# Rank counts in two single-pass products a batch, spare products in the opening's waits, and one spare product a step in attention's last group

## The chip, the cores and the metric

The kernel runs on one core of one Trainium2 chip. The metric is device microseconds of that core, the median of several runs. The engines are TensorE (PE, its weight loads are listed as PEld), VectorE (DVE), ScalarE (ACT), GpSimd (POOL) and SyncE (SP). They run side by side and meet at semaphores.

## The reference

Four layers over `x` of 4 x 1024 x 128 (B = 4 batches, L = 1024 rows, D = 128), each added to its input after a layer norm:

```
x = x + _L0_attn_a_ref(_layernorm(x), ...)   # a rotation of each batch, a code-book term, RMS norm
x = x + _L0_ffn_ref(_layernorm(x), router_w, w1, w2)
x = x + _L0_attn_b_ref(_layernorm(x), ...)   # 16 heads of 8, softmax over 1024 keys
x = x + _L0_ffn_ref(_layernorm(x), router_w, w1, w2)
```

The feed-forward layer sends every row to two of eight experts:

```
logits = jnp.einsum('btd,ed->bte', x, router_w)
top_vals, top_idx = jax.lax.top_k(logits, K)          # K = 2
top_w = jax.nn.softmax(top_vals, axis=-1)
h = jnp.square(jax.nn.relu(jnp.einsum('nd,edh->enh', xf, w1)))
y = jnp.einsum('enh,ehd->end', h, w2)
out = ...sum over the two chosen experts of top_w * y
```

## The kernel before

The program is one long instruction list per engine, with stages in this order: an **opening** (first layer norm, the rotation's matrix, the RMS norm, and the routing of batches 0 and 1), **experts(0)** (the first feed-forward layer), **attention**, and **experts(1)** (the second one).

**Routing of one batch.** `turn_rows` turns the normed rows (`hbs`, tiles of 128) by transposes, ACT copies them out of PSUM, `batch_router` multiplies them by the router weights (`router`, eight products of 8 columns), and DVE copies the logits (`batch_top_two`), finds the largest two and marks them: `mark_two` writes `both`, 8 tiles x 8 experts of 0 or 1, with 8 zero columns behind. `batch_rank` (L1675) then counts on TensorE, for each row and expert, how many rows stand ahead. `rank_lines` (L1666) does that with one product by `tri` (a triangle of ones: rows ahead in the same tile) and eight products by `ones` (rows of all tiles ahead), product d shifted by d tiles and 8 columns narrower each time. All nine are fp32 and each shows as two weight loads and two matmuls in the trace. DVE turns the counts into destinations (`first_lines`, `line_places`), and POOL then **sends** the batch: 16 indirect DMAs that scatter `hbs` to `xs` in DRAM (L547). SP loads the sorted lines back (`load_lines`), and later POOL **fetches** the results by 16 indirect DMAs a batch (L553). A rank is taken eight times: batches 0 to 3 for each of the two feed-forward layers; in the second layer batch 0's lies inside attention (`fill_for_max`, task "rank"), batch 1's in the last group (`routed_late`), 2 and 3 in experts(1).

**experts(f)** walks 48 pairs of line tiles: `turn_lines` (L1704), `lines_hidden` (L1715, 256 columns, fp32), DVE's relu (`relu_pair`, L1332), `units_turned` (L1726), ACT's square (L903), `lines_result` (L1740).

**Attention** walks 16 groups of 16 steps (`STEPS`). A step s (kk is its place in the group) has four score products on 32 rows each (`scores`, L1896, 512 columns), ACT's four exponentials (L1008), sixteen products by the values (`times_values`, L1925), and for a later step the first pass over the scores for their maxima (`first_pass`, L1909, read by DVE's L1442). The first pass runs 13 steps ahead (`AHEAD`), so it ends three steps into the last group, and `routed_late(kk)` puts the routing of batches 1 and 2 of the second feed-forward layer in its place. PSUM slots for DVE (`sm`) alternate in the order of `bank_order`; slot `("out", 2 * GROUPS - 3)` is read at kk = 3 of the last group.

The order on each engine is that in which the code is written; nothing schedules it.

Of the kernel before, what the change touches and what calls it, by code (L numbers as in the profile page):

```python
# [14 lines left out]
P = 128  # L15
# [116 lines left out]
def hybrid_layer(nc, a, out):  # L132
    AR, DR = bank_order()
    ctx = ExitStack()
    with ctx:
# [40 lines left out]
        tri = sb("tri", [P, P])  # L176
# [61 lines left out]
        both = sb("both", [P, (TPB + 1) * E])  # L238
# [781 lines left out]
        def _(dve):  # L1020
# [80 lines left out]
            dve.memset(both[:, TPB * E:(TPB + 1) * E], 0.0)  # L1101
# [159 lines left out]
            def mark_two():  # L1261
                io = iota[:, 0:E].rearrange("p (o e) -> p o e", o=1).broadcast_to([P, TPB, E])
                for k in range(2):
                    ins = dve.tensor_tensor(hot[:, k], io, ixfb[:, :, k:k + 1].broadcast_to([P, TPB, E]), ALU.is_equal)
                link(ins)
                return dve.tensor_tensor(both[:, 0:TPB * E].rearrange("p (t e) -> p t e", e=E), hot[:, 0], hot[:, 1],
                                         ALU.add)
# [274 lines left out]
        def _(pe):  # L1542
# [123 lines left out]
            def rank_lines(bank, parts=(0, 1)):  # L1666

                if 0 in parts:
                    pe.matmul(bank, tri[:], both[:], start=True, stop=False, skip_group_check=True)
                for part in parts:  # L1670
                    for d in range(TPK * part + 1, TPK * (part + 1) + 1):
                        ins = pe.matmul(bank[:, d * E:], ones[:], both[:, 0:(TPB + 1 - d) * E], start=False,  # L1672
                                        stop=(d == TPB), skip_group_check=True)
                return ins
# [111 lines left out]

            def experts_begin():
# [9 lines left out]
                pe.wait_ge(G_("cbb_ready"), 1)  # L1797
                for u in range(2):
                    turn_rows(0, 0, u)
                pe.wait_ge(G_("wqk_loaded"), 48)  # L1800
                batch_router(0, 0)
                second_rows(NBLK - 1)
                batch_rank(0, 0)
                for u in range(2):
                    turn_rows(0, 1, u)
                batch_router(0, 1)
                batch_rank(0, 1)
                pe.wait_ge(G_("w1_loaded"), 16)
                pe.wait_ge(G_("w2_loaded"), 16)

            def routed_late(kk):
# [9 lines left out]
                elif kk in (13, 14):  # L1821
                    batch_router(1, 2, (kk - 13,))

# [156 lines left out]
            for s in range(STEP0, STEP1):  # L1980
# [18 lines left out]
                if s // STEPS == GROUPS - 1:  # L1999
                    routed_late(s % STEPS)  # L2000
# [69 lines left out]
```

## Time and profile before

| | us |
|---|---|
| median of 3 runs | 1381.24 (1376.31 to 1381.48) |
| the profiled execution, its own time | 1387.96 |
| its span | 1386.1 |
| PE busy, PEld busy | 1099.2, 634.3 |
| DVE, ACT, POOL busy | 891.8, 767.9, 540.6 |
| mean granted TensorE clock | 0.865 of full |

The times in rows are microseconds from the span's start. In the timeline a row gives start, duration, engine, line, operation, tiles written and read, shape and count; in brackets stands how long the engine had been idle and what ended that. "remote" there, and "another core or an unknown queue" in the chain, is a wait whose end no instruction of the trace explains. A granted clock of 1.00 is 2.4 GHz, 0.50 is 1.2 GHz; these are the only two levels in the trace.

### The profile page before, as it was taken

Reading aid. Unit: us, or ns where it says so; the run is one execution under the profiler, and the core shown is the slowest. Engines: PE = TensorE matmul, PEld = TensorE weight load, DVE = VectorE, ACT = ScalarE, POOL = GpSimd, SP = SyncE. Lnnn points to the kernel's source line nnn. Section 1 sums busy time; section 2 is a strip of 40 time slices with the busy share of each in tenths; the row PEclk is TensorE's granted clock in tenths of the full one; section 3 lists DMA queues with packets and bytes.
Section 4 is the critical chain, followed back from the end, with each engine's and each line's share of the span. In section 5 each row is a group of like instructions: output and inputs, shape, how many; then the busy total and the mean of one; then the engine's idle time right before and its main releaser. Section 6 shows DMA issues by size and latency. Waiting matters only on the chain.

```text
span 1386.1 us, 23924 instructions
## 1 busy us (share of the span) xinstructions
PE 1099.2 (79%) x8950; PEld 634.3 (46%) x8950; DVE 891.8 (64%) x1819; ACT 767.9 (55%) x1508; POOL 540.6 (39%) x626
## 2 busy tenths in 40 slices
PE   2745765698799999999999999999999688666660
PEld 1444664586233434343444444344343337655560
DVE  6584421346788899998888898888899214223132
ACT  3311221243288888888878888888889322212220
POOL 2035435426745543243424333333221441235344
PEclk9856877797599999999999999999999558778885
DMA  5602313132000000000000000000000102132323
GB/s 192 194 16 79 93 53 104 52 104 61 22 9 9 2 1 2 1 1 1 1 2 1 2 1 2 1 1 1 1 2 2 61 31 85 49 96 65 99 62 109
DMA packets 74863, 57.87 MB, mean 42 GB/s; under 512 B 7676, under 2 KB 68223, under 8 KB 74623
## 3 DMA queue, kind: packets, MB, share of 16 engines
q1 hardware_dynamic: 66558, 39.55, 9.6%
q0 software_dynamic: 8192, 16.79, 4.1%
q8 instruction: 74, 1.21, 0.4%
q14 instruction: 39, 0.31, 0.1%
HBM read 27.68 MB, written 28.57 MB: 41 GB/s over the span
## 4 chain that ended last, share of the span: by engine, by line
PE 58%; DVE 19%; another core or an unknown queue 9%; issue 7%; ACT 4%; POOL 1%; DMA 1%; SPq 0%; POOLq 0%; DVEq 0%; ACTq 0%
PE acc L1925 16%; DVE mxp L1442 10%; PE six L1896 9%; PE six L1715 5%; PE misc L1896 5%; PE six L1726 3%; PE acc L1740 3%; ACT PB L1008 2%; PE six L1740 2%; PE six L1909 1%; PE six L1636 1%; PE six L1704 1%; PE six L1862 1%; PE six L1672 1%
## 5 line engine op out<-in xcount | busy, mean ns | idle before, releaser
L1442 DVE TENSOR_REDUCE mxp<-six 128x2 f32<-128x1024 f32 x512 | 599.0, 1219 | 82.9 <-PE six L1909 71.9
L1008 ACT ACTIVATE PB<-six 128x512 f32<-128x512 f32 x675 | 381.9, 599 | 94.9 <-PE six L1896 47.3
L1925 PE MATMUL acc<-PB,Vg 128*32 128x256 f32 x4096 | 340.8, 405 | 21.4 <-ACT SC L995 14.5
L1896 PE MATMUL six<-Q,K 32*128 32x512 f32 x675 | 280.5, 511 | 4.4 <-issue 4.3
L1909 PE MATMUL six<-K,Q 32*128 32x512 f32 x1024 | 264.3, 516 | 19.5 <-DVE mxp L1442 12.6
L1332 DVE TENSOR_SCALAR PB<-six 128x512 f32<-128x512 f32 x96 | 63.9, 669 | 292.0 <-PE six L1715 135.3
L1008 ACT ACTIVATE PB<-misc 128x512 f32<-128x512 f32 x349 | 208.8, 598 | 51.3 <-PE six L1896 26.4
L903 ACT ACTIVATE PB<-six 128x512 f32<-128x512 f32 x96 | 55.8, 581 | 298.5 <-remote 172.0
L547 POOL DMA_INDIRECT xs<-hbs,dest x128 | 123.8, 967 | 155.9 <-DVE dest L1305 119.2
L1896 PE MATMUL misc<-Q,K 32*128 32x512 f32 x349 | 178.3, 511 | 7.6 <-ACT PB L1008 6.8
L1896 PEld LDWEIGHTS six<-Q,K 32*128 32x128 f32 x675 | 111.8, 187 | 154.6 <-issue 80.0
L637 POOL TENSOR_TENSOR tr<-SC,cst 128x512 fp32r<-128x512 f32 x64 | 66.7, 1042 | 287.3 <-ACT SC L862 287.3
L1925 PEld LDWEIGHTS acc<-PB,Vg 128*32 128x32 f32 x4096 | 83.5, 110 | 151.5 <-issue 82.9
L1726 PE MATMUL six<-cst,PB 128*128 128x128 f32 x368 | 64.7, 303 | 103.1 <-issue 48.8
L553 POOL DMA_INDIRECT hbs<-yd,dest x96 | 91.6, 954 | 108.1 <-issue 91.2
L1909 PEld LDWEIGHTS six<-K,Q 32*128 32x128 f32 x1024 | 97.6, 188 | 35.3 <-DVE mxp L1442 24.3
L1715 PE MATMUL six<-w1s,VH 128*128 x368 | 107.0, 415 | 3.4 <-issue 3.1
L1726 PEld LDWEIGHTS six<-cst,PB 128*128 128x128 f32 x368 | 50.2, 156 | 120.5 <-issue 69.1
L1896 PEld LDWEIGHTS misc<-Q,K 32*128 32x128 f32 x349 | 65.3, 187 | 82.0 <-ACT PB L1008 50.5
L1715 PEld LDWEIGHTS six<-w1s,VH 128*128 128x128 f32 x368 | 69.5, 211 | 10.6 <-issue 4.4
L1740 PE MATMUL acc<-w2s,PB 128*128 x384 | 61.1, 311 | 1.8 <-issue 1.8
L1740 PEld LDWEIGHTS acc<-w2s,PB 128*128 128x128 f32 x384 | 57.0, 227 | 0.7 <-issue 0.7
(310 smaller groups left out, 1307.7 us busy)
## 6 DMA issues: line engine op xcount, KB each, us to landing
yd<-PB SPq DMA_DIRECT2D x40, 256.0 KB
xs<-turned SPq DMA_DIRECT2D x4, 1472.0 KB, 12.2
K<-xs SPq DMA_DIRECT2D x20, 256.0 KB
Q<-xs SPq DMA_DIRECT2D x20, 256.0 KB
x<-in_x SPq DMA_DIRECT2D x4, 512.0 KB, 6.9
SC<-in_w_om SPq DMA_DIRECT2D x1, 2048.0 KB, 12.9
xs<-hbs,dest POOLq DMA_INDIRECT x128
out<-x SPq DMA_DIRECT2D x8, 256.0 KB
```

The lines of the kernel that those rows point to most:

```text
L547: pl.indirect_dma_start(xs[b], bass.IndirectOffsetOnAxis(ap=dest[:, b, k, i:i + 1], axis=0), hbs[:, b, i, :], None).then_inc(G_(f"sent{b}" ...
L553: pl.indirect_dma_start(lines_back[b][:, k, i, :], None, yd[b], bass.IndirectOffsetOnAxis(ap=dest[:, b, k, i:i + 1], axis=0)).then_inc(G_( ...
L637: pl.tensor_tensor(tr[:, task % 2, :], qf[:, task % 2, :], mask.broadcast_to([P, BLK]), ALU.mult).then_inc(G_("high_masked"), 1)
L1008: act.activation(PB[:, s % 3, j, :], scores, ACT.Exp).then_inc(G_("act_taken"), 1)
L1332: dve.tensor_scalar(rls[:, n % 2, 0:w], big[:, n % 2, 0:w], 0.0, None, ALU.max).then_inc(G_("rlp_done"), 1)
L1442: dve.reduce_max(dst, taken_slot("max", s, i).rearrange("p (a n) -> p a n", a=2), AX.X).then_inc(G_("max_taken"), 1)
L1715: ins = pe.matmul(big[:, n % 2, r % 2 * HID:(r % 2 + 1) * HID], hTs[:, group % 2, r % TG * P:(r % TG + 1) * P], w1s[:, ds(expert_at[b, r], ...
L1726: ins = pe.transpose(unit_bank[:, k * P:(k + 1) * P], rls[:, n % 2, k * P:(k + 1) * P], ident)
L1740: ins = pe.matmul(result_bank(group)[:, r % TG * D:(r % TG + 1) * D], sqs[:, n % 3, at:at + P], w2f[:, ds(expert_at[b, r] + c * D, D)], st ...
L1896: pe.matmul(bank, K[rows, G % NG, t * P:(t + 1) * P], Q[rows, G % NG, u * BLK:(u + 1) * BLK], start=True, stop=True).then_inc(G_("act_fill ...
L1909: ins = pe.matmul(slot[:, c * BLK:(c + 1) * BLK], Q[rows, G % NG, t * P:(t + 1) * P], K[rows, G % NG, th * BLK:(th + 1) * BLK], start=True ...
L1925: ins = pe.matmul(acc[RB * j:RB * (j + 1), n], Vg[:, G % 2, t, j, :], PB[:, s % 3, j, n], start=(t == 0 and half == 0), stop=(t == TPB - 1 ...
```

## The change

There are three parts.

**Ranks.** `mark_two` writes `marks` (fp32r, 8 zero columns ahead and behind the 64) and then, by three more adds on DVE, sums over two, four and eight tiles: `twos`, `fours`, `ahead`. `rank_lines` is then two products of 72 columns in fp32r: `tri` by `marks` and `ones_r` by `ahead`, one in each part. `tri` becomes fp32r. In the opening one memset becomes two memsets and two copies.

**Spare products in the opening.** `spare_rows(count, width)` multiplies rows of `hTa` into PSUM bank `six[:, 1]` (fp32, 512 or 256 columns); nobody reads them. The first eight come behind a wait for the second block of the RMS norm (`t_ready` 2), ahead of the first `turn_rows`.

**Spare products in the last group.** `keep_awake` is one fp32r product of 512 columns from kk = 4 on, 12 in all, ahead of `routed_late`; at kk = 4 PE waits for the slot to be read.

```diff
@@ mark_two
-                return dve.tensor_tensor(both[:, 0:TPB * E].rearrange("p (t e) -> p t e", e=E), hot[:, 0], hot[:, 1],
-                                         ALU.add)
+                n = TPB * E
+                link(dve.tensor_tensor(marks[:, E:E + n].rearrange("p (t e) -> p t e", e=E), hot[:, 0], hot[:, 1], ALU.add))
+                marked = marks[:].bitcast(F32)
+                link(dve.tensor_tensor(twos[:, 2 * E:], marked[:, E:E + n], marked[:, 0:n], ALU.add))
+                link(dve.tensor_tensor(fours[:, 4 * E:], twos[:, 2 * E:], twos[:, 0:n], ALU.add))
+                return dve.tensor_tensor(ahead[:, E:], fours[:, 4 * E:], fours[:, 0:n], ALU.add)
@@ rank_lines
-                    pe.matmul(bank, tri[:], both[:], start=True, stop=False, skip_group_check=True)
-                for part in parts:
-                    for d in range(TPK * part + 1, TPK * (part + 1) + 1):
-                        ins = pe.matmul(bank[:, d * E:], ones[:], both[:, 0:(TPB + 1 - d) * E], start=False,
-                                        stop=(d == TPB), skip_group_check=True)
+                    ins = pe.matmul(bank, tri[:], marks[:, E:], start=True, stop=False, skip_group_check=True)
+                if 1 in parts:
+                    ins = pe.matmul(bank, ones_r[:], ahead[:], start=False, stop=True, skip_group_check=True)
@@ new
+            def spare_rows(count, width=BLK):
+                for _ in range(count):
+                    pe.matmul(six[:, 1, 0:width], hTa[:, 0:P], hTa[:, 0:width], start=True, stop=True)
@@ experts_begin, PE
+                pe.wait_ge(G_("t_ready"), 2)
+                spare_rows(8)
                 for u in range(2):
                     turn_rows(0, 0, u)
+                    spare_rows(1, BLK // 2)
...
                 batch_rank(0, 0)
+                spare_rows(8)
                 for u in range(2):
                     turn_rows(0, 1, u)
+                    spare_rows(1, BLK // 2)
                 batch_router(0, 1)
+                spare_rows(3)
                 batch_rank(0, 1)
+                spare_rows(4)
@@ attention's steps, PE
+                    if s % STEPS == 4:
+                        pe.wait_ge(*max_taken("out", 2 * GROUPS - 3))
+                    if s % STEPS >= 4:
+                        keep_awake()
                     routed_late(s % STEPS)
@@ new
+            def keep_awake():
+                bank = sm[:, DR["out", 2 * GROUPS - 3] % 2, 0:BLK]
+                pe.matmul(bank, wkh[:, 0, :], hTh[:, 0:BLK], start=True, stop=True)
```

TensorE in the opening before, from the rank of batch 0 to the first lines of experts(0). `tr` holds the turned rows, `K` the sorted lines:

```order
L1669 MATMUL six<-both,tri 128x72
L1672 MATMUL six<-both,ones 128x64
...
L1672 MATMUL six<-both,ones 128x8
L1647 MATMUL misc<-cst,hbs 128x128 x8
L1652 MATMUL six<-rwf,tr 128x8 x8
L1669 MATMUL six<-both,tri 128x72
L1672 MATMUL six<-both,ones 128x64
...
L1672 MATMUL six<-both,ones 128x8
L1690 TENSOR_LOAD tw
L1704 MATMUL six<-cst,K 128x128 x4
```

The same stretch now (L1799 are the spare products, reading `hTa`, which lies in `PB`):

```order
L1680 MATMUL six<-marks,tri 128x72
L1682 MATMUL six<-ahead,ones_r 128x72
L1799 MATMUL six<-PB 128x512 x8
L1658 MATMUL misc<-cst,hbs 128x128 x4
L1799 MATMUL six<-PB 128x256
L1658 MATMUL misc<-cst,hbs 128x128 x4
L1799 MATMUL six<-PB 128x256
L1663 MATMUL six<-rwf,tr 128x8 x8
L1799 MATMUL six<-PB 128x512 x3
L1680 MATMUL six<-marks,tri 128x72
L1682 MATMUL six<-ahead,ones_r 128x72
L1799 MATMUL six<-PB 128x512 x4
```

The nine products of each rank have become two, and 15 spare ones (and two halves) stand in this stretch; four of them stand between the second rank and the first lines.

TensorE in the last group before, around the first part of batch 1's rank (`routed_late(10)`):

```order
L1896 MATMUL six<-Q,K 128x512 x2
L1647 MATMUL six<-cst,hbs 128x128 x4
L1669 MATMUL six<-both,tri 128x72
L1672 MATMUL six<-both,ones 128x64
L1672 MATMUL six<-both,ones 128x56
L1672 MATMUL six<-both,ones 128x48
L1672 MATMUL six<-both,ones 128x40
L1925 MATMUL acc<-PB,Vg 32x256 x4
```

And now, with the `keep_awake` product (L1851) ahead of the turned rows:

```order
L1925 MATMUL six<-Q,K 128x512 x2
L1851 MATMUL six<-hTh,wkh 128x512
L1658 MATMUL six<-cst,hbs 128x128 x4
L1680 MATMUL six<-marks,tri 128x72
L1954 MATMUL acc<-PB,Vg 32x256 x4
```

One product of 512 columns came in, four of the five rank products of this part went out.

DVE around the marking of batch 0 before, and now:

```order
L1264 TENSOR_TENSOR hot<-cst,ixfb 128x64 x2
L1266 TENSOR_TENSOR both<-hot 128x64
L1271 TENSOR_SCALAR eds<-ed 128x8
```

```order
L1271 TENSOR_TENSOR hot<-cst,ixfb 128x64 x2
L1274 TENSOR_TENSOR marks<-hot 128x64
L1276 TENSOR_TENSOR twos<-marks 128x64
L1277 TENSOR_TENSOR fours<-twos 128x64
L1278 TENSOR_TENSOR ahead<-fours 128x64
L1282 TENSOR_SCALAR eds<-ed 128x8
```

One add has become four in a chain, ahead of everything else on DVE.

## Rows read from the trace of the kernel before

**Rows 1.** The page, part 4: shares of the chain that ended last
```profile
PE 58%; DVE 19%; another core or an unknown queue 9%; issue 7%; ACT 4%; POOL 1%; DMA 1%; SPq 0%; POOLq 0%; DVEq 0%; ACTq 0%
```
**Rows 2.** Timeline of the opening: routing of batch 0, start, duration, what
```profile
67.10 0.48 PE L1796 MATMUL misc<-Vg,ones 1*128 1x128 f32 x2 [2.54 <-ACT Vg L931]
...
73.87 1.09 PE L1647 MATMUL misc<-cst,hbs 128*128 128x128 f32 x4 [6.29 <-DVE hbs L1232]
...
82.11 0.22 DVE L1253 COPY lgb<-six 128x64 f32<-128x64 f32 x1
...
85.49 0.23 DVE L1266 TENSOR_TENSOR both<-hot 128x64 f32<-128x64 f32 x1
...
85.78 0.70 PE L1669 MATMUL six<-both,tri 128*128 128x72 f32 x2 [3.40 <-DVE both L1266]
...
86.15 3.53 PEld L1672 LDWEIGHTS six<-both,ones 128*128 128x128 f32 x16
...
89.89 0.17 DVE L1289 TENSOR_SCALAR tilesi<-six 128x8 int32<-128x8 f32 x1 [3.65 <-PE six L1672]
...
92.88 1.16 POOL L547 DMA_INDIRECT xs<-hbs,dest  x1 [9.15 <-DVE dest L1305]
```
**Rows 3.** Timeline of the opening: routing of batch 1 and the first relu
```profile
112.84 0.23 DVE L1253 COPY lgb<-six 128x64 f32<-128x64 f32 x1 [8.40 <-remote]
...
124.98 0.98 POOL L547 DMA_INDIRECT xs<-hbs,dest  x1 [9.36 <-DVE dest L1305]
...
128.10 1.29 DVE L1332 TENSOR_SCALAR PB<-six 128x512 f32<-128x512 f32 x2
```
**Rows 4.** Windows: stretch, its length, PE busy (count), granted clock, DMA share, GB/s
```profile
65.00:70.00 5.00, 0.48 (x2) 0.93 0.46 131
...
150.00:155.00 5.00, 5.00 (x38) 0.88 0.17 52
```
```profile
1080.00:1085.00 5.00, 3.34 (x17) 0.50 0.16 54
...
1120.00:1125.00 5.00, 5.00 (x30) 0.50 0.13 42
```
**Rows 5.** Timeline of experts(0): a pair of 256-column products at either clock; a rank
```profile
124.37 1.91 PE L1715 MATMUL six<-w1s,VH 128*128 x4
...
127.40 1.03 PE L1715 MATMUL six<-w1s,VH 128*128 x4
...
153.85 0.34 PE L1669 MATMUL six<-both,tri 128*128 128x72 f32 x2
...
153.97 1.87 PEld L1672 LDWEIGHTS six<-both,ones 128*128 128x128 f32 x16
```
**Rows 6.** The chain that ended last, in the last group: start, duration, what
```profile
1109.49 1.65 PE six L1672 x8
...
1115.66 1.81 PE six L1672 x8
...
1120.21 0.72 PE misc L1896
```
**Rows 7.** Timeline of the last group: POOL's sends and ACT's unexplained waits
```profile
1092.90 0.96 POOL L547 DMA_INDIRECT xs<-hbs,dest  x1 [0.31 <-issue]
...
1096.74 0.60 ACT L1008 ACTIVATE PB<-misc 128x512 f32<-128x512 f32 x1 [8.26 <-remote]
```
```profile
1120.46 0.96 POOL L547 DMA_INDIRECT xs<-hbs,dest  x1 [26.60 <-DVE dest L1305]
...
1139.43 0.96 POOL L547 DMA_INDIRECT xs<-hbs,dest  x1 [0.30 <-issue]
...
1143.32 0.60 ACT L1008 ACTIVATE PB<-six 128x512 f32<-128x512 f32 x1 [7.29 <-remote]
```
**Rows 8.** Timelines of experts(1): a rank at full clock, one with the clock low
```profile
1158.38 1.03 PE L1672 MATMUL six<-both,ones 128*128 128x64 f32 x8
...
1162.34 0.96 PE L1672 MATMUL six<-both,ones 128*128 128x32 f32 x8
```
```profile
1237.72 1.86 PE L1672 MATMUL six<-both,ones 128*128 128x64 f32 x8
...
1243.91 0.96 PE L1672 MATMUL six<-both,ones 128*128 128x32 f32 x8
```
**Rows 9.** POOL's own timeline: first sends or fetches of a series in both expert stages
```profile
162.53 0.97 POOL L547 DMA_INDIRECT xs<-hbs,dest  x1 [15.28 <-DVE dest L1305]
201.61 0.98 POOL L553 DMA_INDIRECT hbs<-yd,dest  x1 [19.13 <-issue]
```
```profile
1169.59 0.96 POOL L547 DMA_INDIRECT xs<-hbs,dest  x1 [29.20 <-DVE dest L1305]
...
1250.33 1.00 POOL L547 DMA_INDIRECT xs<-hbs,dest  x1 [19.52 <-DVE dest L1305]
```

More of the change, by code:

```diff
@@ L175, in hybrid_layer @@
         hbs = sb("hbs", [P, B, TPB, D])
-        tri = sb("tri", [P, P])
+        tri = sb("tri", [P, P], F32R)
         ident = cst[:, C_ID:C_ID + P]
@@ L237, in hybrid_layer @@
         hot = sb("hot", [P, 2, TPB, E])
-        both = sb("both", [P, (TPB + 1) * E])
+        marks = sb("marks", [P, (TPB + 2) * E], F32R)
+        twos = sb("twos", [P, (TPB + 2) * E])
+        fours = sb("fours", [P, (TPB + 4) * E])
+        ahead = sb("ahead", [P, (TPB + 1) * E], F32R)
         upto = sb("upto", [P, E, E])
@@ L1100, in _ @@
             link(dve.tensor_tensor(om_skew[:], s1[0:OD, 1, 0:OD], om_bias[:], ALU.subtract))
-            dve.memset(both[:, TPB * E:(TPB + 1) * E], 0.0)
+            dve.memset(twos[:], 0.0)
+            link(dve.memset(fours[:], 0.0))
+            dve.tensor_copy(marks[:], fours[:, 0:(TPB + 2) * E])
+            dve.tensor_copy(ahead[:], fours[:, 0:(TPB + 1) * E])
             dve.tensor_tensor(upto[:], iota[:, 0:E].rearrange("p (e o) -> p e o", o=1).broadcast_to([P, E, E]),
@@ L1797, in experts_begin @@
                 pe.wait_ge(G_("cbb_ready"), 1)
+                pe.wait_ge(G_("t_ready"), 2)
+                spare_rows(8)
                 for u in range(2):
                     turn_rows(0, 0, u)
+                    spare_rows(1, BLK // 2)
                 pe.wait_ge(G_("wqk_loaded"), 48)
-                batch_router(0, 0)
+                batch_router(0, 0, (0,))
+                spare_rows(1, BLK // 2)
+                batch_router(0, 0, (1,))
                 second_rows(NBLK - 1)
+                spare_rows(1)
                 batch_rank(0, 0)
+                spare_rows(8)
                 for u in range(2):
                     turn_rows(0, 1, u)
+                    spare_rows(1, BLK // 2)
                 batch_router(0, 1)
+                spare_rows(3)
                 batch_rank(0, 1)
+                spare_rows(4)
                 pe.wait_ge(G_("w1_loaded"), 16)
```

## The prediction

> **What bounds the kernel now.** I read the chain that ended last first. TensorE has 58% of it, DVE 19%, and 9% is put down to nothing in the trace [rows 1]. So the mean busy shares decide little; I went by places. The timeline around POOL's indirect DMAs explains the 9%. A series of 16 sends takes about 20 us (from 1120.46 to the end of the last send, 1139.43 + 0.96), and while it runs some engine stops without a cause in the trace and goes on 2.9 us after the last send: ACT at 1096.74 after 8.26 us, with the last send over at 1093.86, and at 1143.32 after 7.29 us, with the last over at 1140.39 [rows 7]. DVE's wait of 8.40 us that ends at 112.84 lies at the end of the first series in the same way [rows 2, 3]. I take from this, as an inference, that **work done during a series is covered, and work between the end of a series and the start of the next is paid in full**. A series of sends starts when DVE has the destinations, which hang on a rank. So for each edit I ask whether it lies between series.
>
> The clock is the second view. It is low from about 69 to 125 us (the first row of [rows 4] shows the fall) and again from 1080 to 1145: 13 windows of 5 us at 0.50, of which the first and one in the middle stand in [rows 4]. In the second of them TensorE is busy 5.00 of 5.00 us and the clock stays at 0.50.
>
> **Rank of batch 0, opening.** Before: `both` ends at 85.72, and DVE reads the counts at 89.89, 4.17 us later [rows 2]. Now: three more adds of 0.23 us [rows 2] with some 0.03 between them, 0.8 us, then two single-pass products of 72 columns. The trace has no such pair. Its nearest rows are the two passes of one fp32 product of 72 columns: 0.34 us at full clock [rows 5] and 0.70 at half [rows 2]; I take 0.6 with the handover. 4.17 - 0.8 - 0.6 = 2.8 us saved (2.7 to 3.0), and the sends at 92.88 hang on it: **-2.8**.
>
> On weights, the trace and a rule differ. The 16 weight loads of the eight `ones` products take 3.53 us at half clock and 1.87 at full [rows 2, 5], 221 and 117 ns each. The Trainium skill, TensorE: Matmul & The Clock Gate, section LDWEIGHTS, prices a load of 128 columns at about 107 ns whatever the clock. By that the 18 loads of this rank would be 1.9 us, and this term about -1.1 in place of -2.8; I go by the rows.
>
> **Rank of batch 1.** DVE computes statistics of batch 2 while TensorE ranks, so the rank is hidden and only the three adds count, on the way to the sends at 124.98 [rows 3]: **+0.8**.
>
> **Ranks in the expert stages.** At full clock a rank is 0.34 + 1.9 us [rows 5]; two products are about 0.5, so 1.7 saved. Batch 2's (153.85) lies between series, with TensorE busy 5.00 of 5.00 us [rows 4] and sends at 162.53 [rows 9]: **-1.7**. Batch 3's lies inside the fetches that begin at 201.61 [rows 9]: 0. In the second layer batch 2's (1158 and 1162 [rows 8]) lies before the sends at 1169.59: **-1.7**. Batch 3's takes 1.86 + 0.96 and its `tri` product, some 3.2 us, before the sends at 1250.33 [rows 8, 9]: **-2.2** (-2.7 less a part for the added DVE work). Any of these can be worth 0 if DVE or ACT is late next; that is the lower bound of each.
>
> **Rank inside attention.** TensorE and DVE are both close to full there; the products give 1.7 and the adds cost 0.8. From +0.8 to -1.7; I take **-0.5**.
>
> **Last group.** What is paid is from ACT's return at 1096.74 to the sends at 1120.46. The chain there is TensorE, at half clock. The rank's 1.65 + 1.81 and its `tri` product, 3.8 us [rows 6], become 0.6: -3.2. Four `keep_awake` products (kk 8 to 11) come in. A score product of the same 512 columns has 0.72 in the chain [rows 6]; 0.43 is its columns at 1.2 GHz. I take 0.6: +2.4. Together **-0.8**. The other eight lie at kk 4 to 7, before and in the first series, and at kk 12 to 15, inside the second: cover is the engine stop of 8.26 and of 7.29 us [rows 7]. If that cover goes they cost 8 x 0.72 = 5.8 more. The one at kk 4 is ahead of the first sends: **+0.4**. The wait at kk 4 is for a slot that DVE reads at kk 3, long before: 0.
>
> **Spare products in the opening.** A pair of 256-column fp32 products takes 1.03 us at full clock and 1.91 at half [rows 5], so one of 512 columns about 0.85 and 1.71 in a row of many. The first eight start behind 67.6 [rows 2]. Before, the clock falls in the window up to 70 us, in which TensorE worked 0.48 of 5 us [rows 4]; with products in that idle time I expect it to stay up, and eight take 6.8 us, to 74.8, against a need at 73.87 [rows 2]. DVE takes the logits only at 82.11 [rows 2], and they are ready 2 us before, so 1 us late costs nothing: 0. The eight behind the first rank end before the rows of batch 1 are ready, the three lie in DVE's unexplained wait. The last four stand ahead of the first lines, 3.4 to 6.8 us; DVE is not ready for the first relu before 128.10 [rows 3], TensorE has 1.8 us to spare there and gains some 1.8 us more at full clock: 0 (to +1.7). The two memsets and copies lie in a wait of DVE: 0.
>
> **Sum.** -2.8 + 0.8 - 1.7 - 1.7 - 2.2 - 0.5 - 0.8 + 0.4 = -8.5 us. I take off a sixth for what DVE or ACT will hold back once TensorE is shorter: -7. The profiled execution took 1387.96, its span and 1.9 us around it, 0.5% above the median; it would become 1381, and the median 1381.24 becomes **1374**.
>
> **The rivals.**
> *The clock comes back early in the last group.* If the added product brings it to 1.00 soon after 1097, the 23 us up to the sends shrink, ACT's exponentials (four of 0.60 us a step [rows 7]) becoming the bound near 15 us: 8 more, **1366**. Against it: busy 5.00 of 5.00 us at 0.50 [rows 4], and the added product takes time of its own.
> *The savings are taken back.* The series of sends and fetches, not the ranks, set the pace, and each saving lengthens an unexplained wait. Then only the opening's 2.8 less 0.8 and the added products count, about **1381**. For it: batch 3's rank already lies in a series.
> *Slower: spare products at half clock with their cover gone.* Places: the first eight in the opening, the four ahead of the first lines, kk 4 to 7 and 12 to 15 of the last group. If the clock falls at 69 us in spite of them, the first eight take up to 13.7 us, to 81.3; the turned rows are then 7.4 us late, 5.4 after the 2 us to spare. The four cost the 1.7 of their bound, and the eight of the last group 8 x 0.72 = 5.8 at half clock if no stop covers them. 1374 + 5.4 + 1.7 + 5.8 = **1387**. It decides from the point where the first eight take over 8 us. For it: the clock is low in both places before [rows 4].
>
> **How the numbers follow.** Forecast 1374 (1369 to 1379) 0.50; clock back early 1366, 0.15; taken back 1381, 0.15; slower 1387, 0.20. About 0.5% (7 us) is what a measurement can tell from no change. The forecast lies at that edge: I give 0.30 of its 0.50 to faster, which with the second case makes 0.45; 0.35 for the same; 0.20 slower. The range takes in the middle of the fast and of the slow case: 1363 to 1387.
>
> **What would show it.** Right: the counts are read under 1.6 us after the marks, the first sends begin near 90, each rank is two matmul records; the clock is 1.00 from 67 us until the second rows; ACT's return in the last group still follows the last send by 2.9 us. Wrong: the first turned rows begin after 76; an unexplained wait at a new place between series, since every engine's instruction list has shifted; or the clock at 1.00 between 1100 and 1120.

## The result

The changed kernel took **1373.72 us** (median of 20 runs, 1367.68 to 1377.32); the kernel before, run beside it, 1381.01 (20 runs, 1369.87 to 1389.49). The ratio is 0.9949, 95% interval 0.9932 to 0.9966: 7.3 us less. The profiled execution took 1372.43 with a span of 1370.6, 1.3 us below its median; that of before was 6.9 above its later median. So of the 15.5 us between the two spans, 8.2 are chance, and where that chance lies in the traces isn't known; my estimate is that a single term can be read to some 2 us at best.

The chain of the changed kernel, from its page, part 4, answers to [rows 1]; the share with no cause in the trace rose from 9 to 11%:

```profile
PE 56%; DVE 20%; another core or an unknown queue 11%; issue 6%; ACT 4%; POOL 1%; DMA 1%; SPq 0%; POOLq 0%; DVEq 0%; ACTq 0%
```

The opening of the changed kernel, from the timelines of TensorE, DVE and POOL (start, duration, line and operation, idle time before it), answers to [rows 2] and [rows 3]:

```profile
66.95 8.83 PE L1799 MATMUL six<-PB 128*128 128x512 f32 x16 [0.36 <-ACT cbb L936]
75.61 0.60 PE L1658 MATMUL misc<-cst,hbs 128*128 128x128 f32 x4
...
80.85 0.22 DVE L1259 COPY lgb<-six 128x64 f32<-128x64 f32 x1
...
84.25 0.22 DVE L1274 TENSOR_TENSOR marks<-hot 128x64 fp32r<-128x64 f32 x1
...
85.31 0.43 PE L1680 MATMUL six<-marks,tri 128*128 128x72 f32 x1 [3.05 <-DVE ahead L1278]
85.54 0.41 PE L1682 MATMUL six<-ahead,ones_r 128*128 128x72 f32 x1
...
86.06 0.17 DVE L1300 TENSOR_SCALAR tilesi<-six 128x8 int32<-128x8 f32 x1 [0.28 <-PE six L1682]
...
89.04 1.16 POOL L550 DMA_INDIRECT xs<-hbs,dest  x1 [6.55 <-DVE dest L1316]
...
111.72 0.22 DVE L1259 COPY lgb<-six 128x64 f32<-128x64 f32 x1 [11.13 <-remote]
...
122.94 0.98 POOL L550 DMA_INDIRECT xs<-hbs,dest  x1 [11.19 <-DVE dest L1316]
```

From the end of the marks (84.47) to the read of the counts (86.06) it is 1.59 us; it was 4.17. The first send came 3.84 us earlier than in [rows 2], but 1.26 of that was there already at the copy of the logits (80.85 against 82.11), which no part of the change explains.

The last group of attention, from POOL's and ACT's timelines, answers to [rows 7]:

```profile
1084.95 0.96 POOL L550 DMA_INDIRECT xs<-hbs,dest  x1 [0.30 <-issue]
...
1088.60 0.60 ACT L1011 ACTIVATE PB<-misc 128x512 f32<-128x512 f32 x1 [10.28 <-remote]
...
1110.88 0.96 POOL L550 DMA_INDIRECT xs<-hbs,dest  x1 [24.97 <-DVE dest L1316]
```

ACT comes back 2.7 us after the last send is over (1085.91) and the next sends follow 22.3 us later; before, these were 2.9 and 23.7. The windows of the changed kernel (stretch, length, busy time and count of TensorE, its weight loads, DVE, ACT and POOL, granted clock, DMA share, GB/s) answer to [rows 4]:

```profile
65.00:70.00 5.00, 3.54 (x7) 1.76 (x8) 4.47 (x30) 1.32 (x10) 0.19 (x1) 0.78 0.34 96
70.00:75.00 5.00, 5.00 (x11) 2.08 (x11) 4.76 (x22) 0.00 (x0) 0.38 (x1) 0.88 0.00 0
...
85.00:90.00 5.00, 4.69 (x7) 2.27 (x8) 4.21 (x22) 0.00 (x0) 0.96 (x1) 0.50 0.01 2
...
95.00:100.00 5.00, 4.66 (x31) 3.63 (x30) 4.66 (x23) 1.19 (x2) 3.78 (x5) 1.00 0.15 52
...
1095.00:1100.00 5.00, 5.00 (x29) 2.04 (x25) 1.09 (x6) 1.97 (x5) 0.00 (x0) 0.50 0.01 3
1100.00:1105.00 5.00, 5.00 (x26) 2.88 (x22) 0.00 (x0) 2.55 (x6) 0.00 (x0) 0.50 0.00 0
```

The chain that ended last in that group, in order of time (start, duration, what), answers to [rows 6]:

```profile
1095.89 0.72 PE six L1851
...
1100.94 0.73 PE six L1851
...
1102.52 0.06 PE six L1680
...
1107.09 0.72 PE six L1851
1107.82 0.06 PE six L1682
```

In the opening the clock comes and goes. In the last group it stays at the 1.2 GHz level from ACT's return to the sends, with a `keep_awake` in each step.

### The profile page after: what moved, and what is told of

Same layout as the page of the kernel before. It is cut to its first block, busy times and chain, and to the rows that moved or that the text cites. A ratio compares the mean times of both kernels' runs of the same rounds, so it can differ in the third digit from the quotient of the medians.

```text
span 1370.6 us, 23835 instructions
## 1 busy us (share of the span) xinstructions
PE 1109.0 (81%) x8892; PEld 622.7 (45%) x8892; DVE 896.8 (65%) x1846; ACT 766.7 (56%) x1508; POOL 539.6 (39%) x626
## 4 chain that ended last, share of the span: by engine, by line
PE 56%; DVE 20%; another core or an unknown queue 11%; issue 6%; ACT 4%; POOL 1%; DMA 1%; SPq 0%; POOLq 0%; DVEq 0%; ACTq 0%
PE acc L1954 16%; DVE mxp L1453 10%; PE six L1925 9%; PE six L1724 5%; PE misc L1925 5%; PE six L1735 3%; PE acc L1749 3%; ACT PB L1011 2%; PE six L1749 2%; PE six L1647 1%; PE six L1891 1%; PE six L1713 1%; PE six L1938 1%; DVE PB L1343 1%
## 5 line engine op out<-in xcount | busy, mean ns | idle before, releaser
L906 ACT ACTIVATE PB<-six 128x512 f32<-128x512 f32 x96 | 55.7, 580 | 286.2 <-remote 163.4
L1925 PEld LDWEIGHTS six<-Q,K 32*128 32x128 f32 x675 | 112.0, 187 | 153.0 <-issue 77.7
L678 POOL TENSOR_TENSOR Q<-turned,Q 128x512 fp32r<-128x512 f32 x32 | 40.8, 1276 | 41.1 <-ACT turned L986 41.1
```

Of the source, the lines that this page charges most:

```text
L1925: pe.matmul(bank, K[rows, G % NG, t * P:(t + 1) * P], Q[rows, G % NG, u * BLK:(u + 1) * BLK], start=True, stop=True).then_inc(G_("act_fill ...
```

## The experiments

**Two kinds of chip.** The result stands on a chip whose engines stop during the series of indirect transfers. Eleven of the twelve experiments ran on two other chips, where they do not, and there the kernel before takes some 1190 us in place of 1381. The last ran on a chip that has the stops, where before takes 1390.73. That was chance, and it made two questions of one: what each part is worth with the stops, and without them.

On the chips without stops, executions of one kernel also fall into two clusters. Of the 78 of before, 37 lie between 1182 and 1193 with a mean granted clock of 0.931, and 41 between 1193 and 1204 with 0.918. The difference of 0.013 over 1190 us is about 30 us at half speed, which is how long the clock is low in the last group in the trace of before from the upper cluster (1198.25). So medians there depend on how many executions fall on which side, and the ratios, made against before's own mixture, do not rank the kernels as the medians do. I read places instead. "Sends (1,0)" are those of the second layer's batch 0, and so on; **D** is the distance from the first of them to the start of the last long series of transfers, 80 in a row, after which the kernel needs 111 to 112 us whatever was done before. Each of these distances is from one profiled execution. "At half clock" is the time that TensorE's granted clock stood at 0.50 between 990 and 1060 us.

| kernel | products of 512 columns in the last group | median, us (runs) | at 1193 or more | at half clock, us | sends (1,0) to (1,1), us | (1,0) to (1,2), us | D, us |
|---|---|---|---|---|---|---|---|
| before | none | 1196.97 (35), 1188.0 (18), 1195.98 (25) | 41 of 78 | 34.2 | 29.5 | 67.3 | 90.7 |
| ranks_only | none | 1190.17 (12) | 2 | 23.8 | 26.4 | 59.4 | 82.8 |
| no_keep | none | 1192.42 (12) | 5 | 30.7 | 26.1 | 62.0 | 85.9 |
| no_keep_b (same) | none | 1187.63 (10) | 2 | 13.6 | 23.8 | 55.5 | 79.5 |
| half_sends | none | 1186.97 (1) | | 20.5 | 25.2 | 58.1 | 81.6 |
| no_spares | one a step | 1188.87 (12) | 4 | 0 | 23.0 | 53.0 | 76.5 |
| after_again | one a step | 1183.84 (10) | 3 | 0 | 23.1 | 53.1 | 76.5 |
| old_ranks | one a step | 1189.10 (12) | 0 | 0 | 24.8 | 56.6 | 81.8 |
| keep_two | two a step | 1187.50 (10) | 0 | 0 | 24.7 | 55.7 | 79.1 |
| keep_early | four in steps 8, 9, 10 | 1185.38 (10) | 0 | 6.8 | 23.9 | 55.5 | 79.0 |
| keep_late | four in steps 12, 13, 14 | 1187.64 (10) | 1 | 10.2 | 25.2 | 56.7 | 80.1 |

In the four kernels with the new ranks and no products the distance (1,0) to (1,2) grows by 0.38 us for each us at half clock, and all four lie on that line within 0.1 us. Followed down to no time at half clock it gives 50.3 us, an estimate; with twelve products and the clock kept it is 53.0 to 53.1. So the products cost some 2.7 us there, and pay where the clock would else be low for more than some 7 us.

D leaves out what lies ahead of it, and there the changed kernel gained nothing on these chips: its first sends of all come 2 us earlier (91.47 in after_again against 93.42 in before_again), but sends (1,0) come 2.2 us later (996.19 against 994.01).

### First set: one part at a time

These expectations were written for a chip with the stops.

**ranks_only**: the changed kernel without the spares and without `keep_awake`.

```
-                pe.wait_ge(G_("t_ready"), 2)
-                spare_rows(8)
...
-                    if s % STEPS >= 4:
-                        keep_awake()
```


> The changed kernel without any spare product: no spare_rows in the opening and no keep_awake in attention's last group; only the ranks in two products. Theory (the ranks carry the gain, the spare products are nearly free or a cost): the first sends begin at about 90 us as in the changed kernel, and the section from ACT's return to the sends of batch 1 in the last group is 2.9 us shorter than in the changed kernel, because four keep_awake products of 0.72 us are gone from a chain at half clock. Time 1371, ratio to before 0.993, so 2 to 3 us better than the changed kernel. Rival (the spare products carry it by the clock): the opening after 67 us stays at 0.50 and loses what they gave, time 1378 to 1381, ratio 0.998 or more.

Measured: 1190.17 us (1183.87 to 1193.83), ratio 0.9967 (0.993 to 1.0004), and by medians 1.3 us above no_spares and 6.3 above after_again, where 2 to 3 us below the changed kernel was expected. D is 7.9 us shorter than before's. Both had lost the clock in the last group, but for 24 us here and 34 there: at 0.38 us for each us that is an estimate of 4 us for the clock, and leaves 4 us for the two ranks that lie in D, those of batches 1 and 2, a part of them at half clock.

**no_keep**: the same with the opening's spares.

```
-                    if s % STEPS >= 4:
-                        keep_awake()
```


> The changed kernel without keep_awake: ranks in two products and the opening's spare products. Theory: as the granted clock was 0.50 in the last group with them too, they only cost 0.72 us each where TensorE is the chain, kk 8 to 11: 2.9 us less between ACT's return and the sends of batch 1. Time 1371, ratio 0.9925. Rival (they are covered, or they keep some stretch at full clock): the same time as the changed kernel, ratio 0.995, or slower.

Measured: 1192.42 us (1184.53 to 1197.92), ratio 1.0001 (0.9959 to 1.0044): not the 0.9925 of the theory. Against ranks_only the spares gave nothing by the times.

**no_spares**: the changed kernel without the opening's spares, with `keep_awake`.

```
-                spare_rows(8)
...
-                spare_rows(4)
```


> The changed kernel without the opening's spare products: ranks and keep_awake. Theory (they lie in waits and the clock they give is spent waiting for VectorE): the first sends begin within 1 us of the changed kernel's, ratio 0.995 as the changed kernel. Rival (the full clock in the opening is worth something): the transposes and the router products of batch 0 run at half clock, 3.4 us of products take twice as long, the first sends come 1 to 3 us later and the ratio is 0.997.

Measured: 1188.87 us (1176.33 to 1201.33), ratio 0.9928 (0.9881 to 0.9975). The first sends come at 91.43, as in after_again (91.47): the theory, not the rival.

**old_ranks**: the kernel before, with its nine products a rank, plus both kinds of spare products.

```
+                pe.wait_ge(G_("t_ready"), 2)
+                spare_rows(8)
...
+                    if s % STEPS >= 4:
+                        keep_awake()
```


> The kernel before with both kinds of spare products and the old ranks in nine fp32 products each. Theory: no gain, since the ranks carry it; keep_awake costs 2.9 us in the last group, the opening's rank now runs at whatever clock the eight products ahead of it leave. Time 1382 to 1385, ratio 1.001 to 1.003. Rival (spare products matter): ratio 0.997 or less.

Measured: 1189.10 us (1185.44 to 1192.93), ratio 0.9978 (0.9944 to 1.0012), between the 1.001 of the theory and the 0.997 of the rival, and the interval holds both. Against after_again, with the clock at 2.4 GHz in both, the sends of batch 1 come 1.7 us later after those of batch 0 and the sends of batch 2 1.8 us later after those of batch 1, with one rank in each stretch: **1.7 to 1.8 us a rank**, the 1.7 of the prediction. The rest of the 5.3 us in D, 1.8, lies between the sends of batch 2 and the last series and stays unexplained; batch 3's rank comes after D's end.

What I had not expected stood in the windows of the last group. ranks_only, without the products:

```profile
1005.00:1010.00 5.00, 4.91 (x30) 2.35 (x30) 3.49 (x32) 3.08 (x7) 3.78 (x5) 0.54 0.15 52
1010.00:1015.00 5.00, 5.00 (x29) 2.17 (x27) 0.31 (x2) 3.15 (x7) 3.78 (x5) 0.50 0.15 52
```

no_spares, with one a step:

```profile
1005.00:1010.00 5.00, 4.62 (x45) 2.04 (x37) 3.55 (x33) 3.51 (x8) 3.78 (x5) 1.00 0.15 52
1010.00:1015.00 5.00, 5.00 (x44) 2.54 (x43) 0.58 (x4) 4.40 (x9) 3.40 (x4) 1.00 0.16 54
```

TensorE is busy 4.6 to 5.0 of 5 us in both, and in the one the clock falls. The prediction had the products as a cost alone.

### Second set: is it the products?

**before_again** and **after_again** are the two kernels unchanged; **no_keep_b** is no_keep once more.

> The kernel before, unchanged, for its trace beside the others of this set. Theory (the clock of attention's last group decides what the changed kernel gains): where the engines do not stop during the first series of sends of the second layer, TensorE falls to the 1.2 GHz level some 10 us after the first send of that group's batch 0 and runs 20 us or more there, as in the kernel with the ranks alone (1008 to 1038 us); the first sends of batches 0 and 1 are about 26 us apart and those of batches 1 and 2 about 33. Rival (the ranks alone decide it): the clock is at 2.4 GHz there. Whether the stops named in the prediction are there at all is read here too: with them a series of 16 indirect transfers is followed by at least 7 us without one in all seven places of the experts' stage of layer 2, and the time is about 1381; without them that stage has one series of 80 transfers, and the time is about 1190.

Measured: 1198.25 us, one run. No stops: the last stage has one series of 80. The clock is at half from 1005 us for more than 30 us, as the theory has it, and D is 90.7. The sends are 29.5 and 37.8 us apart, more than the 26 and 33 expected, which were read from the kernel with the new ranks. From its windows:

```profile
1005.00:1010.00 5.00, 5.00 (x32) 1.70 (x26) 1.51 (x15) 2.30 (x6) 3.78 (x5) 0.50 0.17 56
...
1020.00:1025.00 5.00, 5.00 (x33) 1.67 (x32) 3.53 (x17) 2.10 (x4) 1.22 (x2) 0.50 0.04 12
```


> The changed kernel, unchanged. If there are no stops: the clock stays at 2.4 GHz through attention's last group, the second layer's sends of batches 0, 1 and 2 start about 23 and 30 us apart, and the time is 8 us (0.7%) below before's, within 4; the rival (four products a batch is all cost, 0.6 to 0.7 us each) expects 2 to 3 us more than the same kernel without them. If there are stops, as in the profiles shown: 7 us (0.5%) below before's, and the clock does not come back before the second series ends.

Measured: 1183.84 us (1181.64 to 1200.83), ratio 0.9968 (0.9919 to 1.0018), 4.2 us below before's 1188.0 by medians and not clear of noise, so the 8 us are not shown by the times; the sends are 23.1 and 30.0 us apart as expected. From its windows:

```profile
1005.00:1010.00 5.00, 4.62 (x36) 2.78 (x36) 2.90 (x30) 4.28 (x10) 3.83 (x4) 1.00 0.17 56
...
1020.00:1025.00 5.00, 5.00 (x44) 2.96 (x36) 0.83 (x4) 3.77 (x9) 3.78 (x5) 1.00 0.66 189
```


> The changed kernel without the one product of 512 columns a step in attention's last group; the spares of the opening and the new ranks stay. Theory without stops: the clock is lost from about 1008 us for 20 us or more, and the kernel is 3 to 9 us slower than the changed one. With stops: the clock is lost with and without the products, they are a cost of 0.72 us each, and this kernel is about 3 us faster than the changed one. Rival (the products never matter): within 1 us of the changed one.

Measured: 1187.63 us (1184.16 to 1194.54), ratio 0.9999 (0.9954 to 1.0044), 3.8 us above after_again by medians, D 3.0 longer. The clock was lost at 1005 us again, but came back after some 7 us and was lost once more: without the products the loss has no fixed length (D 79.5 here, 85.9 in the same kernel of the first set), which fits the 6 us between the two profiles of one kernel.

### Third set: how many, and where

**keep_two**: two products a step.

```
                         keep_awake()
+                        keep_awake()
```


> Two products of 512 columns a step in attention's last group in place of one, the rest as in the changed kernel. On a chip without stops each product takes 0.34 us of TensorE's path at 2.4 GHz, so twelve more cost 4.1 us. Theory (the products hold the clock, and the executions of the changed kernel near 1198 us are those in which it was lost all the same): no execution is 10 us above the fastest, the median is 1187, from 1185 to 1189, against 1184 for the changed kernel, clock at 2.4 GHz from 1000 to 1045 us. Rival (those executions have another cause): some 3 in 10 stand 12 us above the rest as with one product. With stops: the clock still does not come back before the second series of sends ends, and the time is 3 us above the changed kernel's for some four more products at 0.72 us.

Measured: 1187.50 us (1182.65 to 1189.65), ratio 0.995 (0.9908 to 0.9991): the 1187 of the theory, and no execution of ten at 1193 or more. The clock is at 2.4 GHz from 1000 to 1045 us in the profiled execution. The price of one product at full clock is read from TensorE's timeline of after_again:

```profile
1005.54 0.50 PE L1851 MATMUL six<-hTh,wkh 128*128 128x512 f32 x1
1005.87 0.95 PE L1663 MATMUL six<-rwf,tr 128*128 128x8 f32 x8
```

0.33 us from start to start, 4 us for twelve; keep_two's median is 3.7 us above after_again's. That the second product is what keeps executions away from 1198 us is not shown: old_ranks, with one product a step, has none of 12 at 1193 or more, and the kernels with the new ranks and no products have 9 of 34.

**keep_early**: ranks_only with the twelve products in steps 8, 9 and 10.

```
-                    if s % STEPS >= 4:
-                        keep_awake()
+                    if s % STEPS in (8, 9, 10):
+                        for _ in range(4):
+                            keep_awake()
```


> The new ranks without the opening's spares; the products of 512 columns not one a step but four in each of steps 8, 9 and 10 (as many, twelve), which is about 1005 to 1013 us, where the kernel without products loses the clock. Theory (what decides is that TensorE has wide products where the clock falls): the first loss at 1005 us does not come or comes some us later, the clock may fall after 1018 us, and the first two series of sends are 24 us apart. Rival (any twelve products do): at 2.4 GHz all through, as with one a step, series 23 us apart.

Measured: 1185.38 us (1181.70 to 1189.54), ratio 0.9979 (0.9941 to 1.0016), none of ten at 1193 or more. The clock holds at 1005 us and falls at 1020, and the first two series are 23.9 us apart, all as in the theory. From its windows:

```profile
1005.00:1010.00 5.00, 5.00 (x41) 3.07 (x43) 1.08 (x6) 3.37 (x7) 3.78 (x5) 1.00 0.15 52
...
1020.00:1025.00 5.00, 5.00 (x31) 2.90 (x34) 0.00 (x0) 1.89 (x4) 3.77 (x5) 0.52 0.12 42
```

**keep_late**: the same with `(12, 13, 14)`.

> The same with the twelve products in steps 12, 13 and 14, about 1018 to 1024 us, after the place at which the clock is lost. Theory: it falls near 1005 us as without products and stays at 1.2 GHz at least to 1013 us; the first two series of sends are 26 us apart or more; the time is 3 to 9 us above that of the kernel with the products in steps 8 to 10. Rival (any twelve do): the same as that kernel within 1 us.

Measured: 1187.64 us (1182.90 to 1193.07), ratio 0.9952 (0.991 to 0.9994). The first two series are 25.2 us apart, a little under the 26 expected. The clock falls at 1005 us, is back at 1014.7, before the first of the products at 1018.28, and then stays up. From its windows, and from TensorE's timeline:

```profile
1005.00:1010.00 5.00, 5.00 (x32) 1.72 (x27) 2.20 (x18) 2.30 (x6) 3.78 (x5) 0.50 0.15 52
...
1015.00:1018.00 3.00, 3.00 (x31) 1.23 (x29) 1.52 (x8) 2.47 (x6) 0.00 (x0) 1.00 0.41 124
...
1020.00:1025.00 5.00, 5.00 (x46) 2.90 (x42) 0.80 (x4) 2.57 (x6) 3.78 (x5) 1.00 0.21 67
```
```profile
1018.28 1.20 PE L1842 MATMUL six<-hTh,wkh 128*128 128x512 f32 x4
```

So the products did not bring the clock back: it came back without any, as in no_keep_b (1011.8) and half_sends (1013.4). What they did is keep it there. All profiled kernels of the chips without stops agree on this. At 1005 us the six without such products up to that point lost the clock (before_again, ranks_only, no_keep, no_keep_b, half_sends, keep_late) and the five with them did not. Between 1020 and 1030 us it is low, for a part or all of that time, in the five kernels without them and in keep_early, whose products are over by then, and at 1.00 in the five that have them there, keep_late among them. What counts is the place; "any twelve do" falls, though by times keep_early and keep_late are only 2.3 us apart, less than the 3 to 9 expected and within their spread.

**half_sends**: ranks_only, and of the 16 sends of batch 1 in the second layer only eight.

```
+                if f and b == 1:
+                    last = TPB // 2
```

The two waits that count these transfers are lowered by as much.

> The new ranks alone (no spares, no products in attention's last group), and of the 16 sends of batch 1 in the second layer only the first 8: rows of four of its eight tiles are not sent, so that part of the output is left out. Theory on a chip without stops (from batch 2's sends on, GpSimd's issue of 80 transfers, 1.27 us each, paces the end, and what goes before only shifts its start): the series of batch 1 takes 10 us instead of 20; the last series starts at the usual distance from batch 2's sends, and the kernel is 0 to 4 us faster than with all sends, since batch 2's rank and router, not POOL, are late there. Rival (POOL's transfers pace attention's last group too): 10 us faster. With stops: the engines stop 10 us instead of 20 after this series began, and the time falls by 10 us.

Measured: 1186.97 us, one run, against 1190.17 for all sends, within the 0 to 4 us expected. The next series starts 33.0 us after, as in ranks_only (32.9), though POOL had been free for 23 us:

```profile
1050.79 0.96 POOL L552 DMA_INDIRECT xs<-hbs,dest  x1 [23.19 <-DVE dest L1318]
```

So POOL's series does not pace attention's last group. The experts' stage after it is another matter. POOL's timeline of after_again, its first and one of its last transfers:

```profile
1072.70 1.00 POOL L556 DMA_INDIRECT hbs<-yd,dest  x1 [3.55 <-issue]
...
1173.99 0.94 POOL L556 DMA_INDIRECT hbs<-yd,dest  x1 [0.30 <-issue]
```

There the series lasts 102.2 us in before_again and in after_again, so the rank of batch 3 inside it gives nothing.

### Fourth: two products and no spares, on a chip with stops

**two_no_spares**: keep_two without the opening's spares.

```
-                spare_rows(8)
...
                         keep_awake()
+                        keep_awake()
```


> The changed kernel with two products of 512 columns a step in attention's last group in place of one, and without the opening's spares. Theory (the opening's clock buys nothing, since DVE's chain and the 16 transfers of a series pace the sends there, and what it would save before 100 us is taken back in the first layer's experts): the mark reads still come 1.6 us after the counts' marks, the first series of sends starts within 1 us of the kernels with spares (90 to 92.5 us), the clock is at 1.2 GHz from 80 to 100 us, and the median is that of the kernel with spares and two products, 1187.5, within 2 us. Rival (the spares carry the opening): first sends 2 us later and the median 1189.5 or more. Both expect no execution 10 us above the fastest. With stops: 3 us below before's time.

Measured: 1381.24 us (1379.56 to 1385.63, 6 runs) against 1390.73 for before beside it: ratio **0.9942** (0.992 to 0.9964), the same gain as the change as a whole on its chip, and 9.5 us where 3 were expected. The counts are read 1.59 us after the marks and the first sends start at 91.77, as the theory has it. From its timelines, DVE in the opening and ACT in the last group:

```profile
111.67 0.22 DVE L1259 COPY lgb<-six 128x64 f32<-128x64 f32 x1 [8.35 <-remote]
```
```profile
1093.91 0.60 ACT L1011 ACTIVATE PB<-misc 128x512 f32<-128x512 f32 x1 [8.25 <-remote]
```

And its windows of the last group, to be set beside those of the changed kernel above:

```profile
1100.00:1105.00 5.00, 5.00 (x26) 2.17 (x21) 1.75 (x12) 1.94 (x4) 0.00 (x0) 0.50 0.00 0
1105.00:1110.00 5.00, 5.00 (x43) 2.41 (x41) 0.00 (x0) 3.75 (x8) 0.00 (x0) 0.91 0.01 3
1110.00:1115.00 5.00, 5.00 (x41) 2.18 (x45) 3.47 (x17) 3.62 (x8) 0.95 (x1) 1.00 0.00 0
```

With two products a step the clock comes back 12 us after ACT's return, and the sends of batch 1 start 43.1 us after those of batch 0 (1070.9 and 1114.05), against 45.1 with one product and 46.7 in the kernel before, which has none and the old ranks. That is the rival "the clock comes back early"; it gave 2 us in place of 8, since the return came late. That the second product brought it is likely but not shown: it is one trace, on another chip than the changed kernel's.

**The spares of the opening.** They buy nothing there. From the normed rows (`hbs`) to the copy of the logits it is 9.49 us with them (after_again, clock 0.82 to 1.00 from 80 to 95 us) and 9.50 without (no_spares, clock 0.50), and DVE waits for nothing at that copy: its own work sets it. The first sends come at 91.47 and 91.43. In batch 1 they shorten the way from `hbs` to the copy from 7.49 to 6.36 us; with stops DVE waits there for something else in any case, and the copy comes at 111.72 with them and at 111.67 without. Later they cost: from the first sends to those of batch 2 it is 54.4 to 54.5 us in the five kernels with spares on the chips without stops, and 53.1 to 53.2 in the five with the new ranks and no spares. By times they made no gain (no_keep against ranks_only), and with the stops the gain was whole without them, though with a second product a step in the last group.

## Why the prediction was right, point by point

The time (1373.7 for a forecast of 1374), the range and the leaning to faster by a little held. The terms did less well than their sum. They add up to -8.5 us, of which I took off a sixth for no row that I could name; the places in the two traces add up to the 15.5 us between the spans, of which 8.2 are chance. That the median fell on the forecast to 0.3 us is in part luck.

- **Rank of batch 0, -2.8: right.** 4.17 us became 1.59, 2.6 saved; on the chips without stops 4.17 (before_again) became 1.58 (no_spares). With the price that the Trainium skill, TensorE: Matmul & The Clock Gate, section LDWEIGHTS, gives a load of 128 columns, the term would have been an estimate of -1.1; the 221 ns a load at half clock and the 2.6 us saved decide against that.
- **Rank of batch 1, +0.8: right without the spares.** From the copy of the logits to the first send it is 13.7 us in before_again (106.02 to 119.76) and 14.3 in no_spares (104.04 to 118.36); with the stops 12.1 in [rows 3] and 12.9 in two_no_spares (111.67 to 124.61). In the changed kernel's own trace it is 11.2, the other sign; why stays open.
- **Ranks in the expert stages, -1.7 and -1.7 for batch 2: right in size.** From batch 1's sends to batch 2's it is 1.5 us less in the first layer and 1.6 in the second (0.8 and 1.2 in two_no_spares).
- **Batch 3's ranks, 0 and -2.2: both mis-sized, and the 0 is a step that failed.** In the first layer its rank starts at 205.39, inside the fetches that begin at 201.61 [rows 9], and I took it as covered. From the start of those fetches to batch 3's sends it was 29.9 us (231.50); it is 26.9 in the changed kernel (198.25 to 225.15) and 27.0 in two_no_spares: **3.0 us saved for the 0 forecast**. The place is a relu of DVE behind the stop, ahead of the destinations, first before's, then the changed kernel's:

```profile
229.73 0.69 DVE L1332 TENSOR_SCALAR PB<-six 128x512 f32<-128x512 f32 x1 [2.68 <-PE six L1715]
```
```profile
223.39 0.69 DVE L1343 TENSOR_SCALAR PB<-six 128x512 f32<-128x512 f32 x1
```

Before, TensorE's hidden products for it came only after the stop, and DVE waited 2.68 us; now they are there, in two_no_spares (227.71) too. So work inside a series counts where it decides how far TensorE is when the stop begins. That the shorter rank is what brings it further is likely, but not run by itself. In the second layer it is 4.0 us less from batch 2's sends to batch 3's (3.6 in two_no_spares), and DVE's waits for the same products went from 5.71 and 3.12 us to 3.03 and 1.64.
- **The two new products.** At full clock they start 0.12 us apart and the next product 0.11 after; I had taken 0.5 us for the two.
- **Rank inside attention, -0.5, and the first `keep_awake`, +0.4: not to be read.** From the first layer's batch 3 sends to sends (1,0) it is 1.6 us less of 842 (0.8 in two_no_spares), and the last fetches of the first layer already came 3.3 us earlier by then; attention took 1.7 of that back.
- **Last group, -0.8: right in size, one term mis-sized.** A `keep_awake` costs 0.72 us on the chain, not 0.6. Four lie between ACT's return and the sends, the first at 1090.04 and the others in the chain shown above, so +2.9 in place of +2.4. The two rank products have 0.06 each on the chain, not 0.6 together. Between ACT's return and the sends 1.4 us were saved.
- **Spares, 0: right, with a wrong picture of the clock.** I expected it at 1.00 from 67 us to the second rows. It was 0.78, then 0.88, 1.00 from 75, and 0.50 again from 85 to 90 us. The first eight products took 8.66 us, till 75.61, not 74.8. That is past the 8 us at which the slower rival starts to count, and it still did not come: the last router product ends at 80.17, 0.7 us before DVE takes the logits at 80.85.
- **The stops: the fact held, the rule did not hold everywhere.** ACT's return follows the last send by 2.7 to 3.0 us in the last group of all three traces with stops. DVE's in the opening came 2.5 us after the series in the changed kernel, and in two_no_spares and in [rows 3] 0.3 us before the series ended (at 112.0 and 113.1). That work inside a series is free is not a property of the kernel alone: on two other chips there is no such stop at all.
- **`keep_awake` as a cost alone: right on the chip of the result, wrong on the others.** With the stops and one product a step the clock did not come back, as forecast. On the chips without stops the products cost 0.33 us each at full clock and keep TensorE at 2.4 GHz in the last group, which makes D 3 to 9 us shorter. In the three executions of after_again at 1193 or more the mean clock is 0.931 to 0.934 against 0.944 to 0.947 in the seven others; that it was lost in the last group there is my inference, no trace of such an execution was kept.

What the gain of 7.3 us consists of on the chip with stops is settled only in part. The ranks alone were never run there. That they carry it is inferred from the places above, and from two_no_spares, which excludes the spares but has a second product a step. Nor was the number of rank products run apart from their type: nine became two and fp32 became fp32r at once. What stops the engines stays open, and so does whether it belongs to the chip or to something else that differed there. Loading of instructions does not look like it: the two instruction queues moved 74 and 39 packets in before and 74 and 38 in before_again, and in before none from 1082.5 us to ACT's return at 1096.74. That the clusters are the clock of the last group rests on mean clocks, with a trace of before from the upper one only.

## What to carry to other kernels

Where a result stands ahead of a transfer, replace a series of small accumulating products by sums on a vector engine that would else wait. As I read the rows, weight loads and not columns set the pace of the old series: 16 loads fill 3.53 of its 4.2 us at half clock, and the new pair with three more adds takes 1.6. Products that nobody reads are worth something only where the clock would fall and TensorE is on the path, so look first at where they must stand; where another engine sets the pace, as in the opening, a higher clock buys nothing. Do not put work inside a stop down as free: what an engine gets done before the stop it need not do behind it. And before a wait is explained by the kernel, look whether it is there on a second chip.

## What the runs showed of the hardware

- The same program took 1381 and 1391 us on two chips and about 1190 on two others. Between before's profile of 1386.1 us and before_again's of 1196.4 the difference of 190 us lies where the series of indirect transfers are: 5 us in the opening, 74 in the first expert stage, 110 from attention's last group to the end. Attention in between takes the same to 1 us. There ACT and DVE stop for up to 18.5 us with no cause in the trace, which they never do in before_again. The transfers themselves take the same 1.27 us each in both.
- TensorE fell to 1.2 GHz while the trace has it busy 4.6 to 5.0 of 5 us (no_keep, ranks_only, before_again), and stayed at 2.4 GHz at the same place, where it was no busier, with one product of 512 columns a step added. Once lost, the clock came back by itself after 7 us (no_keep_b) to more than 30 (before_again).
- Executions of the kernel before on one chip lie in two clusters 12 to 13 us apart. How many executions of the other kernels stand at 1193 us or more does not follow the number of products: 9 of 34 with none, 7 of 22 with one a step and the new ranks, none of 12 with one a step and the old ranks, none of 10 with two a step.
